# A graph layer on one core: the turn of the values ahead of layer one, the gelu's copy ahead of the signs, and register loads under the last update

## The chip, the cores and the metric

The kernel runs on one core of one Trainium2 chip. The metric is the device time of one execution in microseconds (us). A core has five engines that run side by side, each through its own instruction stream: TensorE (PE, matmuls), VectorE (DVE), ScalarE (ACT), GpSimd (POOL) and SyncE (SP). They meet only at semaphores: an instruction can wait until a semaphore has reached a value, and everything behind it on the same engine waits with it.

## The reference

6250 nodes with 256 features each, 100,000 edges sorted by their row node. With `xn = layernorm(x)` the reference computes

```python
# graph attention, with L0_gnn_W_w, W_b, a_w, a_b; row = src, col = dst
Wh = xn @ W_w + W_b
e  = f_dst_part[col] + f_row_part[row] + a_b[0];  e = where(e > 0, e, 0.2 * e)
m  = segment_max(e, row);  ex = exp(e - m[row]);  denom = segment_sum(ex, row)
h  = relu(segment_sum((ex / denom[row])[:, None] * Wh[col], row))
# linear attention with 8 heads: q, k = elu(.) + 1, context = k^T v, out @ Wproj^T + bproj
x  = x + h + mix(xn)
# mixture of experts on layernorm(x): router, softmax, top 2 of 8, and for every expert
h = gelu(tokens @ w1[e] + b1[e]);  y = h @ w2[e] + b2[e];  out = out + combine[:, e:e+1] * y
x  = x + moe(layernorm(x))
```

All eight experts are computed for every token, and the weights of the six that were not chosen are zero.

## The kernel before

**Tiles.** The nodes lie in 49 tiles of 128. `xs` holds x for all of them on chip. The edges are put in the order of their row nodes and cut into 904 tiles of 128, two tiles to a group (452 groups), four groups to a slot (113 slots, `GS` is 4). A prologue (the first layernorm, the projections and the table of `Wh` rows in memory) takes the first 520 us. After it all engines run one loop over slots, written out in full, `for s in range(-2, S_END)`; there are no planner and no scheduler, and the order on each engine is the order in which the loop body calls the functions.

**The graph part of a slot.** POOL gathers the `Wh` rows of every edge tile from the table with an indirect DMA (L640, 904 of them, eight to a slot). The ring `G` has room for 16 groups, so the gather of group g waits until `total(g - 16)` has been done on TensorE (semaphore `e_A`). DVE takes a slot's edge scores (`edge_scores`, L1528 to L1536) as soon as `spread` on TensorE has written them (semaphore `e_EX`), builds the one-hot matrices (L1539), multiplies them by the weights (L1547, L1549) and, for the slot after that, by the values (`values`, L1556, semaphore `e_V`). TensorE turns these values with eight transposes (`turn`, L1049, semaphore `e_VT`). DVE takes their maximum (`shifts`, L1561 and four small ones). ACT makes the signs, which are the turned one-hots (`one_hot_turned`, L762, semaphore `e_OT`). TensorE spreads the row quantities over the edges (`spread`, L1067 and L1068), which ends in `e_EX`, and so lets DVE begin the next slot. `total(g)` (L1081 to L1083, six matmuls) sums a group's rows; the slot has two of them at its beginning and two in its middle. DVE adds each to the running sum `U` (`add_up`, L1583). Where a node tile has had its last group, `window_end` divides `U` and adds it to `x`, and reads from tables of numbers which node tile is next and at which group it ends (registers `wid` and `last_group`). There are 49 such ends.

**The expert part.** From slot 50 to slot 153 every slot also has one layer one (`up`, L1215, 12 matmuls of 512 columns) of one expert for four node tiles. ACT takes the gelu of both halves (`hidden`, L843; a table load of the activation engine comes ahead of it), copies it to 16 bits (`hidden_hi`, L851, semaphore `m_hi`), and DVE subtracts the copy from the gelu (`split`, L1745). In the slot after, TensorE does layer two (`down`, L1228 and L1231, in two halves), and in the one after that DVE adds the result (`add`, L1758). In slots 50 to 110 both parts run side by side (61 slots); from slot 111 on only the expert part is left.

Two waits stand at the front of `up`: its operands and the gelu of the slot before (`m_g`). `turn` waits for `e_V`, and the two `total` behind both wait for nothing of this slot.

Of the kernel before, what the change touches and what calls it, by code (L numbers as in the profile page):

```python
# [27 lines left out]
ds = bass.ds  # L28


def graph_layer(nc, x, src, dst, W_w, W_b, a_w, a_b, Wq, Wkv, Wproj, bproj, router_w, w1, b1, w2, b2, out):
# [50 lines left out]
    with ExitStack() as ctx:  # L82
# [562 lines left out]
        def _(act):  # L645
# [212 lines left out]
            for s in range(-2, S_END):  # L858
# [13 lines left out]
                if s in UP_AT:  # L872
                    hidden(*UP_AT[s])
                if s + 2 < NS:
                    one_hot_turned(s + 2)
                    if s in UP_AT:
                        act.activation(ready[:, s:s + 1], epsc[:, :], ACT.Exp)
                if s in UP_AT:
                    hidden_hi(*UP_AT[s])
# [20 lines left out]
        def _(pe):  # L900
# [335 lines left out]
            for s in range(-2, S_END):  # L1236
# [15 lines left out]
                if s in FIRST:  # L1252
                    logits(FIRST[s], s)
                if s in UP_AT:
                    up(*UP_AT[s])
                if s + 2 < NS:
                    turn(s + 2)
# [22 lines left out]
        def _(dve):  # L1280
# [8 lines left out]
            def pause():  # L1289

                dve.memset(idle[:, :], 0.0)
# [227 lines left out]
            dve.reg_load(wid, wids[0:1, 0:1])  # L1519
# [3 lines left out]
            link(dve.memset(mx[:, 1, GS:GS + 1], 0.0))  # L1523

# [61 lines left out]
            def window_end(g):  # L1586

                with dve.If(dve.snap(last_group) == g + 1):
                    w = dve.snap(window, min_val=0, max_val=W - 1)
                    dve.wait_ge(e_U, g + 1)  # L1590
# [8 lines left out]
                    dve.wait_ge(f_x, w + 1)  # L1599
                    pause()  # L1600
                    dve.reg_load(last_group, tendi[0:1, ds(w + 1, 1)])
                    dve.reg_load(wid, wids[0:1, ds(w + 1, 1)])
                    dve.reg_add(window, window, 1)

# [50 lines left out]
            def mixed(p):  # L1655
                n = of_pair[p]
                x_p = xs[:, 2 * p:2 * p + n, :]
                dve.wait_ge(a_pj, p + 1)
                dve.tensor_tensor(x_p, x_p, bank[7][:, 0:n * D].rearrange("p (j c) -> p j c", j=n), ALU.add
                                  ).then_inc(a_x, 1)  # L1660
                dve.wait_ge(a_x, p + 1)


            def norm_stats(b):
                n = of_batch[b]
                for j in range(n):
                    rest(5 * b + j)
                    dve.reg_load(wid_n, wids[0:1, b * NB + j:b * NB + j + 1])
                    x_w = xs[:, ds(dve.snap(wid_n, min_val=0, max_val=W - 1), 1), :].rearrange("p a c -> p (a c)")
                    dve.bn_stats(stats[:, j, :], x_w).then_inc(m_st, 1)  # L1670
# [178 lines left out]
```

## Time and profile before

| | |
|---|---|
| median of 3 runs | 2242.29 us (2235.94 to 2250.9) |
| profiled execution | 2250.89 us |
| its span | 2249.1 us |
| TensorE busy | 1711.7 us (76%) |
| VectorE busy | 1676.1 us (75%) |
| ScalarE busy | 963.0 us (43%) |
| GpSimd busy | 985.1 us (44%) |
| chain that ended last | DVE 41%, PE 25%, issue 17%, unknown queue 8%, ACT 5% |

The profiled execution is the slowest of the three; device time and span differ by 1.8 us. Busy shares are averages over stages that differ: a prologue to about 520 us, slots with graph work alone to 1219 us, slots with graph and expert work to 2004 us, and expert work alone to the end. "remote" as the end of an idle time says that the semaphore came from something the profile doesn't name; "issue" says that nothing visible was waited for.

### The profile page before, as it was taken

Reading aid. Unit: us, or ns where it says so; the run is one execution under the profiler, and the core shown is the slowest. Engines: PE = TensorE matmul, PEld = TensorE weight load, DVE = VectorE, ACT = ScalarE, POOL = GpSimd, SP = SyncE. Lnnn points to the kernel's source line nnn. Section 1 sums busy time; section 2 is a strip of 40 time slices with the busy share of each in tenths; the row PEclk is TensorE's granted clock in tenths of the full one; section 3 lists DMA queues with packets and bytes.
Section 4 is the critical chain, followed back from the end, with each engine's and each line's share of the span. In section 5 each row is a group of like instructions: output and inputs, shape, how many; then the busy total and the mean of one; then the engine's idle time right before and its main releaser. Section 6 shows DMA issues by size and latency. Waiting matters only on the chain.

```text
span 2249.1 us, 40227 instructions
## 1 busy us (share of the span) xinstructions
PE 1711.7 (76%) x13588; PEld 1261.0 (56%) x13588; DVE 1676.1 (75%) x4219; ACT 963.0 (43%) x2291; POOL 985.1 (44%) x988
## 2 busy tenths in 40 slices
PE   3778875641887578888856888887878788889998
PEld 2557562531765466666634555655555555566666
DVE  5999898652666667786667888888788878875665
ACT  6322130211332232222224656565656566656555
POOL 3000003325666666665666666665666656610000
PEclk7899997875999788888877999999999999989999
DMA  5011120113655344433333333333332334930000
GB/s 171 18 55 61 43 72 22 55 44 89 174 162 156 100 124 118 108 101 93 88 83 89 84 91 86 93 84 91 79 93 79 93 78 90 81 40 10 11 20 12
DMA packets 121460, 182.21 MB, mean 81 GB/s; under 512 B 21490, under 2 KB 91902, under 8 KB 121214
## 3 DMA queue, kind: packets, MB, share of 16 engines
q0 software_dynamic: 45312, 120.06, 23.0%
q1 hardware_dynamic: 75904, 59.25, 8.4%
q8 instruction: 111, 1.82, 0.3%
q14 instruction: 133, 1.09, 0.2%
HBM read 152.43 MB, written 26.63 MB: 80 GB/s over the span
## 4 chain that ended last, share of the span: by engine, by line
DVE 41%; PE 25%; issue 17%; another core or an unknown queue 8%; ACT 5%; DVEq 2%; POOL 1%; ACTq 0%; DMA 0%; SPq 0%; POOLq 0%
PE bank L1215 6%; PE bank L1231 5%; DVE mloc L1561 4%; DVE big L1478 3%; DVE scr L1583 3%; DVE big L1745 3%; DVE big L1483 3%; DVE big L1480 2%; DVE work L1758 2%; DVE big L1485 2%; DVE scr L1443 2%; DVE work L1539 2%; DVE work L1556 1%; PE bank L1049 1%
## 5 line engine op out<-in xcount | busy, mean ns | idle before, releaser
L640 POOL DMA_INDIRECT work<-table,tiles x904 | 911.9, 1009 | 573.9 <-PE bank L1083 299.5
L1231 PE MATMUL bank<-big 128*128 128x256 f16 x2352 | 329.9, 281 | 24.5 <-issue 23.2
L1081 PE MATMUL bank<-work,scr 128*128 128x257 f16 x904 | 270.0, 299 | 24.3 <-issue 14.2
L1215 PE MATMUL bank<-scr,big 128*128 128x512 f16 (+1 forms) x1248 | 277.0, 371 | 0.6 <-ACT big L843 0.3
L1082 PE MATMUL bank<-work,scr 128*128 128x256 f16 x904 | 270.6, 299 | 7.0 <-issue 6.6
L1231 PEld LDWEIGHTS bank<-big 128*128 128x128 f16 x2352 | 235.4, 100 | 67.0 <-issue 31.3
L1083 PE MATMUL bank<-work,scr 128*128 128x257 f16 x904 | 268.7, 297 | 3.7 <-issue 3.5
L1583 DVE SCALAR_TENSOR_TENSOR scr<-scr,gg,bank 128x257 f32<-128x257 f32 x452 | 216.6, 479 | 51.3 <-remote 19.1
L762 ACT ACTIVATE work<-bank 128x1024 f16<-128x1024 f16 x113 | 115.7, 1024 | 310.6 <-DVE mloc L1561 211.3
L972 PE MATMUL bank<-big 128*128 128x208 f16 x1568 | 176.9, 268 | 73.1 <-DVE big L1485 54.8
L972 PEld LDWEIGHTS bank<-big 128*128 128x128 f16 x1568 | 150.5, 102 | 99.4 <-issue 94.1
L1049 PE MATMUL bank<-identh,work 128*128 128x128 f16 x904 | 79.3, 239 | 156.8 <-DVE work L1556 109.8
L1745 DVE TENSOR_TENSOR big<-big 128x1024 f16<-128x1024 f32 (+1 forms) x104 | 120.8, 1161 | 100.2 <-ACT big L851 86.5
L1215 PEld LDWEIGHTS bank<-scr,big 128*128 128x128 f16 x1248 | 118.1, 98 | 123.7 <-issue 9.9
L843 ACT ACTIVATE big<-bank,b1c 128x512 f32<-128x512 f32 (+1 forms) x208 | 126.6, 659 | 134.2 <-PE bank L1215 111.3
L1758 DVE SCALAR_TENSOR_TENSOR work<-bank,comb,work 128x256 f32<-128x256 f32 x392 | 169.1, 477 | 7.9 <-issue 7.3
L1049 PEld LDWEIGHTS bank<-identh,work 128*128 128x128 f16 x904 | 62.4, 108 | 188.6 <-DVE work L1556 124.5
L1561 DVE TENSOR_REDUCE mloc<-bank 128x4 f32<-128x1024 f16 x113 | 137.7, 1219 | 35.0 <-PE bank L1049 20.6
L1067 PE MATMUL bank<-tiles,work 128*128 128x2 f16 x904 | 60.3, 165 | 95.9 <-ACT work L762 51.0
L745 ACT ACTIVATE w<-s 128x8 f32<-128x8 f32 x113 | 23.5, 208 | 254.7 <-DVE s L1536 211.9
L1228 PE MATMUL bank<-big,onesq 128*128 128x256 f16 x392 | 109.6, 279 | 23.0 <-DVE work L1758 15.1
L691 ACT COPY big<-bank 128x256 f32<-128x256 f32 x49 | 18.3, 373 | 252.3 <-PE bank L984 230.9
(342 smaller groups left out, 3416.6 us busy)
## 6 DMA issues: line engine op xcount, KB each, us to landing
work<-table,tiles POOLq DMA_INDIRECT x904
scr<-normed_cols SPq DMA_DIRECT2D x98, 128.0 KB
table<-big SPq DMA_DIRECT2D x49, 129.0 KB, 2.2
normed_rows<-scr SPq DMA_DIRECT2D x49, 128.5 KB, 2.8
big<-normed_rows SPq DMA_DIRECT2D x49, 128.5 KB
normed_cols<-big SPq DMA_DIRECT2D x49, 128.0 KB, 1.7
xs<-in_x_dram SPq DMA_DIRECT2D x4, 1536.0 KB, 14.5
out_dram<-work SPq DMA_DIRECT2D x48, 128.0 KB
```

Source lines behind the costliest of these rows:

```text
L640: pool.indirect_dma_start(G[:, r, j, :], None, table, bass.IndirectOffsetOnAxis(ap=col[:, t:t + 1], axis=0)).then_inc(rows_in[r // GS], 16)
L972: mm = pe.matmul(bank[4 + k][:, 0:TT], A[n % 2][:, j // 2, :, j % 2], Bh[n % 2][:, j // 2, :, j % 2], start=(n == BATCH[b] and j == 0), st ...
L1049: mm = pe.transpose(VT[:, j * P:(j + 1) * P], V[:, j // 2, :, j % 2], identh[:, :])
L1081: pe.matmul(of[:, 0:D + 1], hi, Gh[:, r, j, 0:D + 1], start=(j == 0), stop=False)
L1082: pe.matmul(of[:, 0:D], hi, Gh[:, r, j, D + 2:2 * D + 2], start=False, stop=False)
L1083: mm = pe.matmul(of[:, 0:D + 1], lo, Gh[:, r, j, 0:D + 1], start=False, stop=(j == GT - 1))
L1215: mm = pe.matmul(bank[5 + f][:, 0:n * P], w1p[pw][:, e, h, f * P:(f + 1) * P], x2p[b % 2][px][:, h, 0:n * P], start=(h + m == 0), stop=(h ...
L1231: mm = pe.matmul(of, hTp[ph][:, k % 2, f, (j + c) * P:(j + c + 1) * P], w2p[pw][:, e, f, :], start=False, stop=(f == 1 and m == 2))
L1561: dve.tensor_reduce(mloc[:, :], VT.rearrange("p (k e) -> p k e", k=GS), AX.X, ALU.max).then_inc(e_ml, 1)
L1583: dve.scalar_tensor_tensor(U, U, gg[:, g // GS % 4, g % GS:g % GS + 1], bank[3 + g % 2][:, 0:D + 1], ALU.mult, ALU.add).then_inc(e_U, 1)
L1745: dve.tensor_tensor(hTp[1][:, k % 2, :, 0:n * P], hT[:, :, 0:n * P], hTp[0][:, k % 2, :, 0:n * P], ALU.subtract).then_inc(m_lo, 1)
L1758: ins = dve.scalar_tensor_tensor(a_, bank[Y_BANK[i % 2]][:, c * D:(c + 1) * D], comb[:, b % 2, j + c, e:e + 1], a_, ALU.mult, ALU.add)
```

## The change

Three orders are changed, and no arithmetic.

1. ACT copies the gelu (`hidden_hi`) right behind `hidden`, ahead of the signs and of the small Exp, which is there to have its table loaded.
2. TensorE turns the values (`turn(s + 2)`) ahead of layer one (`up`).
3. In `window_end` the two register loads, and the small memset ahead of them (`pause`), go to the start of the branch, where the last update of `U` still runs. The wait for the addition to `x`, at the end of the branch so far, is gone from there: it stands at the branch's start for the addition before, and in `mixed` (25 calls) and `norm_stats` (13 calls), which read `x`, as `windows_added`. A memset at the start gives `f_x` its first count, and `reg_load(wid, ...)` ahead of the loop is gone.

```diff
--- before.py
+++ after.py
@@ -871,12 +871,11 @@
                     norm_scale(FIRST[s + 4])
                 if s in UP_AT:
                     hidden(*UP_AT[s])
+                    hidden_hi(*UP_AT[s])
                 if s + 2 < NS:
                     one_hot_turned(s + 2)
                     if s in UP_AT:
                         act.activation(ready[:, s:s + 1], epsc[:, :], ACT.Exp)
-                if s in UP_AT:
-                    hidden_hi(*UP_AT[s])
                 if s - 2 in A_AT:
                     reciprocals_sb(A_AT[s - 2])
                 for p in K_AT.get(s, ()):
@@ -1251,10 +1250,10 @@
                     norm_turned(FIRST[s + 1], len(halves(FIRST[s + 1])) - 1, s)
                 if s in FIRST:
                     logits(FIRST[s], s)
+                if s + 2 < NS:
+                    turn(s + 2)
                 if s in UP_AT:
                     up(*UP_AT[s])
-                if s + 2 < NS:
-                    turn(s + 2)
                 if 0 <= s < NS:
                     for g in range(GS * s + GS // 2, GS * (s + 1)):
                         total(g)
@@ -1516,11 +1515,11 @@
             window = dve.alloc_register("window")
             wid = dve.alloc_register("wid")
             wid_n = dve.alloc_register("wid_n")
-            dve.reg_load(wid, wids[0:1, 0:1])
             dve.reg_mov(window, 0)
             dve.reg_load(last_group, tendi[0:1, 0:1])
             link(dve.memset(U, 0.0))
             link(dve.memset(mx[:, 1, GS:GS + 1], 0.0))
+            dve.memset(started[:, 3:4], 0.0).then_inc(f_x, 1)
 
             def edge_scores(s):
                 dve.wait_ge(e_EX, s + 1)
@@ -1587,6 +1586,10 @@
 
                 with dve.If(dve.snap(last_group) == g + 1):
                     w = dve.snap(window, min_val=0, max_val=W - 1)
+                    pause()
+                    dve.reg_load(wid, wids[0:1, ds(w, 1)])
+                    dve.reg_load(last_group, tendi[0:1, ds(w + 1, 1)])
+                    dve.wait_ge(f_x, w + 1)
                     dve.wait_ge(e_U, g + 1)
                     dve.tensor_scalar(dn[:, :], U[:, D:D + 1], 1e-30, None, ALU.max).then_inc(f_dn, 1)
                     dve.wait_ge(f_dn, w + 1)
@@ -1596,11 +1599,11 @@
                     dve.wait_ge(f_hh, w + 1)
                     x_w = xs[:, ds(dve.snap(wid, min_val=0, max_val=W - 1), 1), :].rearrange("p a c -> p (a c)")
                     dve.tensor_tensor(x_w, x_w, hh, ALU.add).then_inc(f_x, 1)
-                    dve.wait_ge(f_x, w + 1)
-                    pause()
-                    dve.reg_load(last_group, tendi[0:1, ds(w + 1, 1)])
-                    dve.reg_load(wid, wids[0:1, ds(w + 1, 1)])
                     dve.reg_add(window, window, 1)
+
+            def windows_added():
+
+                dve.wait_ge(f_x, dve.snap(window, min_val=0, max_val=W) + 1)
 
             def keys_one(p):
                 n = of_pair[p]
@@ -1655,6 +1658,7 @@
             def mixed(p):
                 n = of_pair[p]
                 x_p = xs[:, 2 * p:2 * p + n, :]
+                windows_added()
                 dve.wait_ge(a_pj, p + 1)
                 dve.tensor_tensor(x_p, x_p, bank[7][:, 0:n * D].rearrange("p (j c) -> p j c", j=n), ALU.add
                                   ).then_inc(a_x, 1)
@@ -1663,6 +1667,7 @@
 
             def norm_stats(b):
                 n = of_batch[b]
+                windows_added()
                 for j in range(n):
                     rest(5 * b + j)
                     dve.reg_load(wid_n, wids[0:1, b * NB + j:b * NB + j + 1])
```

On ACT, in a slot that has both parts (`ready<-epsc` is the small Exp, `work<-bank` the signs, CAST the copy of the gelu). Before:

```order
L843 ACTIVATE big<-bank,b1c 128x512 [waits m_up]
L843 ACTIVATE big<-bank,b1c 128x512
L762 ACTIVATE work<-bank 128x1024 [waits e_EX,e_ml]
L877 ACT_TABLE_LOAD
L877 ACTIVATE ready<-epsc 128x1
L851 CAST big<-big 128x1024 [waits m_y,m_g]
L745 ACTIVATE w<-s 128x8 [waits e_S,e_s3]
```

and now:

```order
L843 ACTIVATE big<-bank,b1c 128x512 [waits m_up]
L843 ACTIVATE big<-bank,b1c 128x512
L851 CAST big<-big 128x1024 [waits m_y,m_g]
L762 ACTIVATE work<-bank 128x1024 [waits e_EX,e_ml]
L878 ACT_TABLE_LOAD
L878 ACTIVATE ready<-epsc 128x1
L745 ACTIVATE w<-s 128x8 [waits e_S,e_s3]
```

The copy has moved up by three rows, and the signs now stand behind it.

On TensorE, in the middle of such a slot, between the second `total` and the third. Before:

```order
L1083 MATMUL bank<-work,scr 128x257
L1215 MATMUL bank<-scr,big 128x512 [waits m_g,m_xlo]
L1215 MATMUL bank<-scr,big 128x512 x11
L1049 MATMUL bank<-identh,work 128x128 [waits e_OT,e_ml,e_V]
L1049 MATMUL bank<-identh,work 128x128 x7
L1081 MATMUL bank<-work,scr 128x257 [waits e_U,e_S]
```

and now (lines are one lower from here on):

```order
L1082 MATMUL bank<-work,scr 128x257
L1048 MATMUL bank<-identh,work 128x128 [waits e_OT,e_ml,e_V]
L1048 MATMUL bank<-identh,work 128x128 x7
L1214 MATMUL bank<-scr,big 128x512 [waits m_g,m_xlo]
L1214 MATMUL bank<-scr,big 128x512 x11
L1080 MATMUL bank<-work,scr 128x257 [waits e_U,e_S]
```

The transposes, with their wait for `e_V`, now stand ahead of layer one, and the third and fourth `total` are still behind both.

On DVE, behind the update that a node tile ends with (the branch is taken 49 times). Before:

```order
L1588 COMPARE_AND_BRANCH
L1591 TENSOR_SCALAR dn<-scr 128x1
L1592 REGISTER_ALU
L1593 RECIPROCAL rd<-dn 128x1
L1595 TENSOR_SCALAR work<-scr,rd 128x256
L1597 ISA
L1598 TENSOR_TENSOR xs<-xs,work 128x256
L1291 MEMSET idle 128x1
L1601 ISA
L1601 TENSOR_LOAD tendi
L1602 REGISTER_ALU
L1602 TENSOR_LOAD wids
```

and now:

```order
L1587 COMPARE_AND_BRANCH
L1290 MEMSET idle 128x1
L1590 ISA
L1590 TENSOR_LOAD wids
L1591 ISA
L1591 TENSOR_LOAD tendi
L1594 TENSOR_SCALAR dn<-scr 128x1
L1596 RECIPROCAL rd<-dn 128x1
L1598 TENSOR_SCALAR work<-scr,rd 128x256
L1600 ISA
L1601 TENSOR_TENSOR xs<-xs,work 128x256
```

Memset and loads have moved from behind the addition to `xs` to ahead of the first small operation.

## Rows read from the trace of the kernel before

**Rows 1.** The three later stages (window: length, busy by engine, granted clock, DMA share, GB/s).
```profile
524.00:1219.00 695.00, 508.89 (x3709) 393.16 (x3710) 461.67 (x1162) 193.10 (x565) 429.69 (x424) 0.83 0.42 115
1219.00:2004.00 785.00, 633.40 (x5479) 447.37 (x5477) 654.24 (x1769) 482.16 (x935) 470.68 (x468) 0.94 0.40 85
2004.00:2249.00 245.00, 232.00 (x1815) 164.19 (x1813) 149.55 (x410) 142.85 (x212) 0.00 (x0) 0.99 0.04 12
```

**Rows 2.** DVE's edge operation: first and last of 62 starts that bound 61 slots.
```profile
1212.45 0.17 DVE L1528 TENSOR_TENSOR s<-bank,work 128x8 f32<-128x8 f32 x1 [0.87 <-issue]
...
2009.29 0.16 DVE L1528 TENSOR_TENSOR s<-bank,work 128x8 f32<-128x8 f32 x1
```

**Rows 3.** DVE groups, 1219 to 2004 us: busy, mean ns, idle before and its releasers.
```profile
L1583 DVE SCALAR_TENSOR_TENSOR scr<-scr,gg,bank 128x257 f32<-128x257 f32 x240 | 114.9, 479 | 23.0 <-issue 11.4 <-remote 5.4 <-PE bank L1083 2.7
...
L1561 DVE TENSOR_REDUCE mloc<-bank 128x4 f32<-128x1024 f16 x61 | 74.3, 1217 | 22.7 <-PE bank L1049 14.3 <-remote 5.8 <-issue 2.5
L1745 DVE TENSOR_TENSOR big<-big 128x1024 f16<-128x1024 f32 x60 | 73.3, 1221 | 23.4 <-issue 12.8 <-ACT big L851 9.9
```

**Rows 4.** One slot on DVE (start, length, engine, line, idle before).
```profile
1341.71 0.17 DVE L1528 TENSOR_TENSOR s<-bank,work 128x8 f32<-128x8 f32 x1 [0.23 <-remote]
...
1344.13 0.68 DVE L1556 TENSOR_TENSOR work<-work,fdp 128x1024 f16<-128x1024 f16 x1
...
1347.96 1.22 DVE L1561 TENSOR_REDUCE mloc<-bank 128x4 f32<-128x1024 f16 x1 [1.45 <-remote]
...
1352.72 1.23 DVE L1745 TENSOR_TENSOR big<-big 128x1024 f16<-128x1024 f32 x1 [0.90 <-ACT big L851]
1354.05 0.17 DVE L1528 TENSOR_TENSOR s<-bank,work 128x8 f32<-128x8 f32 x1
```

**Rows 5.** The same slot on TensorE.
```profile
1342.43 2.75 PE L1215 MATMUL bank<-scr,big 128*128 128x512 f16 x12
1345.02 0.61 PE L1049 MATMUL bank<-identh,work 128*128 128x128 f16 x8
...
1346.69 0.27 PE L1083 MATMUL bank<-work,scr 128*128 128x257 f16 x1
...
1350.69 0.16 PE L1068 MATMUL bank<-tiles,work 128*128 128x2 f16 x1
```

**Rows 6.** The same slot on POOL: first and last gather of its two bursts.
```profile
1342.20 0.96 POOL L640 DMA_INDIRECT work<-table,tiles  x1 [1.68 <-PE bank L1083]
...
1346.00 0.96 POOL L640 DMA_INDIRECT work<-table,tiles  x1 [0.30 <-issue]
1348.27 0.95 POOL L640 DMA_INDIRECT work<-table,tiles  x1 [1.31 <-PE bank L1083]
...
1352.05 0.96 POOL L640 DMA_INDIRECT work<-table,tiles  x1 [0.30 <-issue]
```

**Rows 7.** The same slot on ACT.
```profile
1345.22 1.27 ACT L843 ACTIVATE big<-bank,b1c 128x512 f32<-128x512 f32 x2 [0.37 <-PE bank L1215]
1349.22 1.02 ACT L762 ACTIVATE work<-bank 128x1024 f16<-128x1024 f16 x1 [2.73 <-issue]
...
1351.66 1.03 ACT L851 CAST big<-big 128x1024 f16<-128x1024 f32 x1
```

**Rows 8.** Two transposes of the values on TensorE behind long idle times.
```profile
1539.83 0.57 PE L1049 MATMUL bank<-identh,work 128*128 128x128 f16 x7 [3.58 <-DVE work L1556]
...
1685.11 1.03 PE L1049 MATMUL bank<-identh,work 128*128 128x128 f16 x8 [4.03 <-DVE work L1556]
```

**Rows 9.** The end of a node tile on DVE.
```profile
1557.94 0.06 DVE L1291 MEMSET idle<- 128x1 f32 x1
1558.87 1.23 DVE L1745 TENSOR_TENSOR big<-big 128x1024 f16<-128x1024 f32 x1 [0.87 <-issue]
```

**Rows 10.** The register loads of one line (times in ns: least, median, most).
```profile
L1601 DVEq TENSOR_LOAD <-tendi x49: 301/309/319, 583.5 to 1941.6; - x49
```

**Rows 11.** A slot of the stage before: last gather and next edge operation.
```profile
762.90 0.95 POOL L640 DMA_INDIRECT work<-table,tiles  x1 [0.30 <-issue]
765.37 0.17 DVE L1528 TENSOR_TENSOR s<-bank,work 128x8 f32<-128x8 f32 x1 [3.14 <-remote]
```

## The prediction, made before the changed kernel ran

> **What bounds the kernel now.** I read the times by stage first [rows 1]. The tail of experts alone has TensorE busy 232 of 245 us at a granted clock of 0.99, and the change only touches its order of copies, so it stays. The stage of slots 50 to 110 is where all three edits meet, and there no engine is full: DVE is busy 654 of 785 us, TensorE 633. So the time of a slot is set by a loop through several engines. Its length is read between two edge operations of DVE (L1528): 2009.29 - 1212.45 = 796.8 us for 61 slots, 13.06 us each [rows 2].
>
> Next, where DVE idles in that stage [rows 3]: 22.7 us ahead of the maximum of the turned values (L1561), of them 14.3 for the transposes; 23.4 us ahead of the split (L1745), of them 9.9 for the copy on ACT. These are the waits that edits 1 and 2 aim at. The 12.8 us "issue" there and 11.4 ahead of L1583 hold the register loads of edit 3.
>
> Then one slot on four engines. In it DVE's edge operation starts at 1341.71; call that e. The values end at e + 3.10 [rows 4]. TensorE, meanwhile, runs `up` from e + 0.72 to about e + 3.3, so it fills just the time in which the values are made, and its transposes start at e + 3.31 and are followed by the last `total`, ending at e + 5.25 [rows 5]. POOL has made four gathers, stopped, starts the other four at e + 6.56 and the last at e + 10.34 [rows 6]. The `spread` that the next edge operation waits for ends at 1350.85 (e + 9.14) [rows 5], but DVE does not begin before 1354.05, e + 12.34, which is 2.00 us after the start of the last gather [rows 4, 6]. In this slot DVE has a late split in between, so I look at one without experts: 762.90 is the last gather, 765.37 the edge operation, with DVE idle for 3.14 us ahead of it and `spread` long over [rows 11]. Over the stage, 37 edge operations come in a pause between two bursts of gathers; 29 of these start 2.0 to 2.8 us behind the start of the last gather, 5 sooner, 3 later. The others come while a burst runs, at the end of DVE's own work. I take it as this: **what TensorE signals reaches the others only about 2 us after the start of the last gather of a burst**. The trace shows the times, not the mechanism.
>
> **Edit 2, the turn ahead of layer one.** It removes from the transposes the wait for `up`, and adds to `up`, and to both `total` behind it, the wait for `e_V`. From the slot above: the values are there at e + 3.10. The transposes need 0.45 until the next matmul can start (1345.02 to 1345.47, of 0.61 in all) [rows 5], `up` 2.59 (1342.43 to 1345.02), and the third `total` about 0.8. The third `total` ends at 3.10 + 0.45 + 2.59 + 0.8 = e + 6.9, the fourth near 7.6, against 5.25 now. TensorE stands still from about e + 0.4 to e + 3.1, where it did `up` before. Gathers restart at about e + 7.4 instead of 6.56; the last of the four starts 3 x 1.26 = 3.78 later, at 11.2; with 2.0 more the next edge operation is at **e + 13.2**. No slot with four gathers behind the third `total` can be shorter.
>
> How much that costs depends on how many slots are shorter now. Of the 61 lengths, whose ends are in [rows 2], 34 are below 13.2 (the shortest 10.55), and raising these to 13.2 gives 42.4 us; to 13.7, 60.8 us (43 slots); to 14.0, 74.3.
>
> The granted clock pushes upward. Ten times in this stage the transposes stand behind at least 2.2 us of idle TensorE; six of these ran at the full clock, as after 3.58 us idle, and four at half of it, 1.03 us instead of 0.61 [rows 8]. The change makes such an idle time in nearly every slot. Where the transposes run at the half clock (1.2 instead of 2.4 GHz) they lose 0.42 us, and some of `up` behind them up to as much as its own length, 2.6. With four in ten, and 0.4 to 2 us each, the mean is 0.2 to 0.8; I take 0.5, and so 13.7 us: **+61 us**, with bounds +42 (full clock always) and +119 (14.9 us, half clock in every slot for most of `up`).
>
> The Trainium skill, "TensorE: Matmul & The Clock Gate", the section on HAM oscillation, says of a loop in which each step computes for a short while and then waits that the engine starts cold at every step. The rows agree only in part: four of ten.
>
> **Edit 1, the copy ahead of the signs.** Copy 1.03 us, signs 1.02, table load and Exp 1.4 between them [rows 7]. The copy is ready 2.4 us earlier behind the gelu. The gelu now starts with `up` at about e + 6.2 and ends at e + 7.5 to 7.8, the copy at 8.9, the signs at 9.9, `spread` near 10.5. The split at 9.9 finds its copy. The signs were ready to go at e + 5.9 and are pushed back by 3 us; that costs nothing as long as 10.5 is ahead of 13.2, and if the gathers did not hold the edge operation, it would be behind a DVE chain of 10.55 by little. So the edit is worth at most the 9.9 us of waits for the copy [rows 3], and only in slots that the floor above does not set.
>
> The same goes for the waits for the transposes, 14.3 us. If 18 of 61 slots are longer than 13.7, the share of both is (14.3 + 9.9) x 18 / 61 = **-7 us**.
>
> **Edit 3, the register loads.** Behind a node tile's addition come the memset and 0.87 us in which DVE does nothing [rows 9]; in it lie two loads of 0.31 [rows 10]. Under the update (0.48 us) they hide in part: bounds 0 and -0.93, and I take -0.4, since a load pair is longer than what is left of the update when the branch is decided. Some 24 of the 49 ends lie before slot 50 and 25 in the stage. In the slots without experts DVE waits for the edge operation anyway, 3.14 us in the one shown [rows 11], so few of them count: -2. In the stage 18/61 of 25 ends: 7 x 0.4 = **-3 us**. The 38 new waits for the last addition find it done; 0 to +0.1 each, taken as 0. What covers them is the same wait on edges.
>
> The Trainium skill, "DMA: Bandwidth & Descriptors", in "Latency and other measured facts", gives a floor of about 600 ns for one `tensor_load`; the rows have 0.31. By its figure an end would give 1.2 instead of 0.6 us of loads, an estimate; the trace decides.
>
> **Sum.** 61 - 7 - 3 - 2 = +49 us. On the profiled execution 2250.9 + 49 = 2300; that execution is the slowest of three, and against their median it is 2242.3 + 49 = 2291, rounded to **2292 us**. The bounds of this case alone: +28 (full clock, 42 less 14) to +70, that is 2270 to 2312.
>
> **Rivals.**
> *A, faster: nothing holds the edge operation.* If the 2 us behind the gathers are a coincidence of DVE's own work, only the waits count. The maximum finds its values turned (-14.3 and half the remote 5.8), the split its copy (-9.9, of which the later gelu gives back half), and 25 window ends give 10: about -28, **2214 us**. It decides if edge operations can start, in most slots, at less than 1.5 us behind the last gather of a burst. For it: the five that do, and the 24 that come while a burst runs. Against it: the 29, and the slot in which DVE is empty and `spread` done [rows 11]. Chance 0.17.
>
> *B, the same: gain and loss meet.* The floor is 13.2 at full clock or less, because the third `total` alone restarts POOL earlier than I put it (at e + 7.0, 16.6 to 29.8 us for floors of 12.3 to 12.8), and the waits of all longer slots go, with -12 to -20. This gives 0 to +18: **2250 us**. Chance 0.2.
>
> *C, the clock falls in every slot.* In the stage without experts, with TensorE busy 509 of 695 us, the clock is 0.83 against 0.94 [rows 1]. If the idle time of every slot brings the half clock for the turn and for most of `up`, the slot is 14.9 us: +119 - 5, **2355 us**. Against it: the six transposes at full clock. Chance 0.1.
>
> **Numbers.** Forecast 0.53, A 0.17, B 0.2, C 0.1. 1% of 2242 is 22 us, about what a measurement of this kernel can tell from no change: 2220 to 2265. Faster gets A less a little at its edge, 0.16; the same gets B's greater part and the edges of A and the forecast, 0.2; slower the rest, 0.64. The range of 8 in 10 runs from 2220, at the inner edge of A, to 2342, short of C.
>
> **What would show it.** In the trace of the changed kernel: the stage takes about 835 us instead of 785, with the same busy times. Transposes start 0.1 us after the values, behind 2.5 to 3 us of idle TensorE that names L1555 or so as releaser, over 130 us in the stage. L1560, the maximum, waits for next to nothing. The first gather of the second burst starts near e + 7.4, and the edge operation 2.0 to 2.7 us after the last. The stage's clock falls from 0.94 to 0.88 to 0.92. The prediction is wrong if edge operations come without regard to the gathers, if POOL's second burst still starts near e + 6.6, or if the slots that are longer than 13.7 us now shrink by more than the 10 us I give them.

## The result, and the profile after

The changed kernel takes **2293.78 us** (median of 6 runs, 2276.84 to 2306.23) against 2240.69 us (6 runs, 2235.94 to 2259.52) for the kernel before in the same comparison: ratio 1.0213, interval 1.0181 to 1.0245. It is slower beyond its interval; whether by more or by less than 2% the interval doesn't decide. The profiled execution has a span of 2304.5 us, 55.4 more than before. Ratios are of undisturbed executions: one of the eleven of the changed kernel run again later took 3179 us and is not in its ratio.

The time is in the stage in which graph and expert work meet. Windows of the changed kernel, as in [rows 1] (window: length, busy PE, PEld, DVE, ACT, POOL, granted clock, DMA share, GB/s):

```profile
524.00:1219.00 695.00, 508.66 (x3708) 394.36 (x3707) 463.36 (x1167) 193.06 (x566) 430.31 (x425) 0.83 0.42 115
1219.00:2060.00 841.00, 654.42 (x5487) 449.93 (x5486) 655.01 (x1771) 482.85 (x936) 468.53 (x468) 0.91 0.37 79
2060.00:2304.00 244.00, 230.88 (x1810) 163.01 (x1807) 147.22 (x403) 142.17 (x211) 0.00 (x0) 1.00 0.04 12
```

The stages around it have hardly moved: 2.2 us less up to the first of the edge operations below, 1.9 us more behind the last. DVE and ACT have the same busy time, TensorE has 21 us more at a clock of 0.91 instead of 0.94. The edge operations that bound the 61 slots, to compare with [rows 2]:

```profile
1210.26 0.17 DVE L1527 TENSOR_TENSOR s<-bank,work 128x8 f32<-128x8 f32 x1 [1.91 <-remote]
...
2062.77 0.17 DVE L1527 TENSOR_TENSOR s<-bank,work 128x8 f32<-128x8 f32 x1 [0.31 <-PE bank L1067]
```

852.5 us instead of 796.8, that is 13.98 us for a slot instead of 13.06: +55.7, the whole loss. DVE's groups in this stage (busy, mean ns, idle before and releasers), the same lines as in [rows 3] and the edge operation:

```profile
L1582 DVE SCALAR_TENSOR_TENSOR scr<-scr,gg,bank 128x257 f32<-128x257 f32 x241 | 115.6, 480 | 60.1 <-PE bank L1082 49.6 <-remote 7.3 <-issue 0.7
...
L1750 DVE TENSOR_TENSOR big<-big 128x1024 f16<-128x1024 f32 x60 | 73.1, 1219 | 5.3 <-ACT big L851 4.3
L1560 DVE TENSOR_REDUCE mloc<-bank 128x4 f32<-128x1024 f16 x60 | 72.9, 1216 | 2.6 <-remote 2.6
...
L1527 DVE TENSOR_TENSOR s<-bank,work 128x8 f32<-128x8 f32 x60 | 9.9, 166 | 69.8 <-remote 53.0 <-PE bank L1067 16.6
```

The waits that the change aims at are gone: 22.7 to 2.6 ahead of the maximum, 23.4 to 5.3 ahead of the split. Two others have taken their place: the updates of `U` wait 60.1 us (23.0 before), 49.6 of it for a `total`, and the edge operation waits 69.8.

There are two kinds of slot now (e is again the start of the slot's edge operation). In the first TensorE keeps its full clock. Turn and layer one; then the last gather of the first burst, and the first and last of the second; then DVE's edge operations:

```profile
1421.90 0.62 PE L1048 MATMUL bank<-identh,work 128*128 128x128 f16 x8 [1.86 <-DVE work L1555]
1422.36 2.76 PE L1214 MATMUL bank<-scr,big 128*128 128x512 f16 x12
```

```profile
1423.63 0.95 POOL L640 DMA_INDIRECT work<-table,tiles  x1 [0.30 <-issue]
1426.05 0.95 POOL L640 DMA_INDIRECT work<-table,tiles  x1 [1.47 <-PE bank L1082]
...
1429.83 1.55 POOL L640 DMA_INDIRECT work<-table,tiles  x1 [0.30 <-issue]
```

```profile
1418.69 0.17 DVE L1527 TENSOR_TENSOR s<-bank,work 128x8 f32<-128x8 f32 x1 [1.95 <-remote]
...
1431.84 0.17 DVE L1527 TENSOR_TENSOR s<-bank,work 128x8 f32<-128x8 f32 x1 [1.29 <-remote]
```

The second burst starts at e + 7.36, the last gather at e + 11.14, the next edge operation at e + 13.15, 2.01 us behind it. In the second kind the clock falls in the wait for the values:

```profile
1355.38 1.03 PE L1048 MATMUL bank<-identh,work 128*128 128x128 f16 x8 [2.50 <-DVE work L1555]
1356.21 5.21 PE L1214 MATMUL bank<-scr,big 128*128 128x512 f16 x12
```

Layer one takes 5.21 us instead of 2.76. On ACT the gelu, the copy and the signs follow it in a row, and on DVE the edge operation starts at 1366.61, 14.34 us after the one at 1352.27, released by the `spread` (L1067) and not by a gather (the last one started at 1366.19):

```profile
1361.46 1.26 ACT L843 ACTIVATE big<-bank,b1c 128x512 f32<-128x512 f32 x2 [6.05 <-PE bank L1214]
1362.76 1.05 ACT L851 CAST big<-big 128x1024 f16<-128x1024 f32 x1
1363.71 1.02 ACT L762 ACTIVATE work<-bank 128x1024 f16<-128x1024 f16 x1
```

```profile
1366.61 0.17 DVE L1527 TENSOR_TENSOR s<-bank,work 128x8 f32<-128x8 f32 x1 [1.54 <-PE bank L1067]
```

It comes 1.27 us after the end of this `spread`. In ten of the 61 slots it is 1.27 to 1.35 us behind it, so in them the 2 us behind the last gather are not what DVE waits for.

Both traces have the same 61 slots, so each can be set beside itself. Layer one takes more than 3.2 us in 32 of them (5 before). These 32 took 406.9 us and take 461.3: 12.71 us each before, 14.42 now, +54.5 in sum. The other 29 took 390.0 and take 391.2: 13.45 each before, 13.49 now, +1.2. So nearly the whole loss lies in the slots in which layer one met the half clock. They were the shorter slots before, so this does not yet say how much of it is the clock and how much the order.

### The profile page after: what moved, and what is told of

Same layout as the page of the kernel before. It is cut to its first block, busy times and chain, and to the rows that moved or that the text cites. A ratio compares the mean times of both kernels' runs of the same rounds, so it can differ in the third digit from the quotient of the medians.

```text
span 2304.5 us, 40290 instructions
## 1 busy us (share of the span) xinstructions
PE 1732.0 (75%) x13588; PEld 1264.4 (55%) x13588; DVE 1675.2 (73%) x4220; ACT 963.0 (42%) x2291; POOL 982.6 (43%) x988
## 4 chain that ended last, share of the span: by engine, by line
DVE 33%; PE 31%; issue 15%; another core or an unknown queue 12%; ACT 5%; DVEq 2%; POOL 1%; ACTq 0%; DMA 0%; SPq 0%; POOLq 0%
PE bank L1214 11%; PE bank L1230 4%; DVE big L1477 3%; DVE mloc L1560 3%; DVE big L1482 2%; PE bank L1048 2%; DVE big L1479 2%; DVE big L1484 2%; DVE work L1555 2%; DVE scr L1582 2%; DVE big L1750 2%; DVE work L1538 2%; PE bank L1134 2%; ACT work L762 2%
## 5 line engine op out<-in xcount | busy, mean ns | idle before, releaser
L1214 PE MATMUL bank<-scr,big 128*128 128x512 f16 (+1 forms) x1248 | 326.3, 419 | 0.4 <-ACT big L843 0.3
L1230 PE MATMUL bank<-big 128*128 128x256 f16 x2352 | 314.9, 274 | 13.8 <-issue 13.5
L1048 PE MATMUL bank<-identh,work 128*128 128x128 f16 x904 | 90.3, 259 | 248.7 <-DVE work L1555 193.7
L1080 PE MATMUL bank<-work,scr 128*128 128x257 f16 x904 | 264.5, 293 | 5.1 <-DVE scr L1582 2.6
L1081 PE MATMUL bank<-work,scr 128*128 128x256 f16 x904 | 265.0, 293 | 2.6 <-issue 2.5
L1082 PE MATMUL bank<-work,scr 128*128 128x257 f16 x904 | 262.8, 291 | 3.7 <-issue 3.7
L1230 PEld LDWEIGHTS bank<-big 128*128 128x128 f16 x2352 | 229.7, 98 | 49.6 <-issue 18.7
L971 PE MATMUL bank<-big 128*128 128x208 f16 x1568 | 175.9, 267 | 72.5 <-DVE big L1484 55.4
L1048 PEld LDWEIGHTS bank<-identh,work 128*128 128x128 f16 x904 | 67.9, 117 | 272.9 <-DVE work L1555 212.2
L1214 PEld LDWEIGHTS bank<-scr,big 128*128 128x128 f16 x1248 | 129.8, 109 | 154.5 <-issue 68.0
L971 PEld LDWEIGHTS bank<-big 128*128 128x128 f16 x1568 | 149.8, 102 | 99.5 <-issue 94.5
L1527 DVE TENSOR_TENSOR s<-bank,work 128x8 f32<-128x8 f32 x113 | 18.6, 165 | 170.9 <-remote 149.0
L1066 PE MATMUL bank<-tiles,work 128*128 128x2 f16 x904 | 60.1, 166 | 90.8 <-ACT work L762 51.8
L1477 DVE TENSOR_TENSOR big<-tiles,scr 128x1664 f16<-128x1664 f16 x98 | 99.9, 1019 | 33.3 <-PE bank L971 18.8
```

Source lines behind the costliest of these rows:

```text
L971: mm = pe.matmul(bank[4 + k][:, 0:TT], A[n % 2][:, j // 2, :, j % 2], Bh[n % 2][:, j // 2, :, j % 2], start=(n == BATCH[b] and j == 0), st ...
L1048: mm = pe.transpose(VT[:, j * P:(j + 1) * P], V[:, j // 2, :, j % 2], identh[:, :])
L1080: pe.matmul(of[:, 0:D + 1], hi, Gh[:, r, j, 0:D + 1], start=(j == 0), stop=False)
L1081: pe.matmul(of[:, 0:D], hi, Gh[:, r, j, D + 2:2 * D + 2], start=False, stop=False)
L1082: mm = pe.matmul(of[:, 0:D + 1], lo, Gh[:, r, j, 0:D + 1], start=False, stop=(j == GT - 1))
L1214: mm = pe.matmul(bank[5 + f][:, 0:n * P], w1p[pw][:, e, h, f * P:(f + 1) * P], x2p[b % 2][px][:, h, 0:n * P], start=(h + m == 0), stop=(h ...
```

## The experiments

They ran on four chips (numbers 0, 2, 5 and 7), and on all of them the kernel before takes **2064 us**, not 2241. The number of the first comparison's chip is not on record. Each run was compared with the kernel before on its own chip. Most of the expectations were written for a kernel of 2241 us, so they are read here as ratios. The first thing to read is therefore the kernel before, traced again on one of them (no edit).

> The kernel before, traced. Where it takes 2064 us, the stage without experts has slots of 11.0 us instead of 12.96, edge operations do not wait 2 us behind the last gather of a burst, and POOL's bursts run into each other; the idle time ahead of the edge operation named remote, 104.6 us in the first trace, is below 10. Where it takes 2240 us, they are as in the first trace.

2061.28 us, a span of 2059.5. The idle time ahead of the edge operation (L1528, whole span), by releaser:

```profile
  issue: 14.6, 17
  PE bank L1068: 1.6, 2
```

No idle time named remote is left there, nor ahead of the edge operation in any other trace of the experiments. Slots take 12.25 us in the mean instead of 13.06, those without experts 11.1 instead of 13.0, and of 61 edge operations two come 1.9 to 2.9 us behind the last gather, where in the first trace it was 30. The very first edge operation shows it best. In the first trace 32 gathers run without a pause, and this is the end of the first `spread`, the last of these gathers, and the edge operation:

```profile
525.77 0.17 PE L1068 MATMUL bank<-tiles,work 128*128 128x2 f16 x1
```

```profile
548.22 0.95 POOL L640 DMA_INDIRECT work<-table,tiles  x1 [0.31 <-issue]
```

```profile
550.91 0.17 DVE L1528 TENSOR_TENSOR s<-bank,work 128x8 f32<-128x8 f32 x1 [25.75 <-issue]
```

and on the other chip, where the gathers go on from 487.7 to beyond 529:

```profile
504.39 0.17 PE L1068 MATMUL bank<-tiles,work 128*128 128x2 f16 x1
```

```profile
504.08 0.95 POOL L640 DMA_INDIRECT work<-table,tiles  x1 [0.30 <-issue]
505.34 1.25 POOL L640 DMA_INDIRECT work<-table,tiles  x1 [0.31 <-issue]
```

```profile
504.59 0.17 DVE L1528 TENSOR_TENSOR s<-bank,work 128x8 f32<-128x8 f32 x1 [0.81 <-PE bank L1068]
```

There it starts 0.03 us after `spread` has ended, in the middle of a burst; in the first trace it comes 25 us after `spread` and 2.7 behind the last gather. So the hold on which the prediction rests belongs to the chip of the first comparison, or to a state it was in; the program is the same. The difference of the two spans, 189.6 us, is 46 to the first edge operation, 94 in the slots without experts, and 49 in the 61 with them.

**The change on such a chip** (no edit).

> The changed kernel itself, on the chips on which the kernel before takes 2064 instead of 2241 us and on which halving the gathers of the kernel before gave nothing. From the parts on those chips (order alone +113 us, copy -23, loads -25): 2064 + 65 = 2110 to 2140 us, 3% slower, more than the 2.1% where edge operations are held behind the gathers. Theory that the second burst of gathers matters there too in the changed kernel (with half the gathers it took 2060): second bursts start at e + 7.3 or e + 8.9, and the next edge operation waits for the totals. If the change cost only through the hold of the edge operation, it would be the same here, 2050 to 2075 us.

2070.73 us (11 runs), ratio 1.0029 (1.0020 to 1.0038). Neither 2110 to 2140 nor its reason came true: the loss is 6 us where edge operations aren't held. That lies in the range given for the case that the change costs only through the hold. But edit 2 costs here too, and edits 1 and 3 pay for it, as the next runs show; the parts do not add up. What DVE waits for in the stage (1067 to 1820 us; us in total, times, longest):

```profile
DVE scr L1582 <- PE bank L1082: 22.7, 25, 2.8
DVE w4l L1543 <- ACT w4h L746: 17.6, 13, 1.9
...
DVE big L1750 <- ACT big L851: 2.8, 9, 0.5
```

**The turn back behind layer one**: edits 1 and 3 stay.

```diff
-                if s + 2 < NS:
-                    turn(s + 2)
                 if s in UP_AT:
                     up(*UP_AT[s])
+                if s + 2 < NS:
+                    turn(s + 2)
```

> Edits 1 and 3 with the turn back behind layer one. My theory (the second burst of gathers waits for the third total, and the edge operation for the gathers): the loss of the change goes wholly, about 2240 less what the waits and the register loads give, so 2215 to 2240 us; POOL's second burst starts at e + 6.6 again. The rival, that the loss comes from the signs behind the copy (spread late, edge operation late): 2275 to 2295 us, as the signs stay where the change has put them.

2019.17 us against 2063.79, ratio 0.9788 (0.9771 to 0.9804). It beats both kernels. As a ratio 0.988 to 1.0 was expected, and it is better. With the full change at 1.0029, edit 2 on top of the other two costs 2.4%, some 50 us. The waits of the same stage:

```profile
DVE dn L1594 <- DVE scr L1582: 9.3, 13, 0.8
DVE xs L1601 <- DVE work L1598: 4.1, 26, 0.2
...
DVE work L1555 <- ACT fdp L754: 3.3, 2, 1.8
DVE mloc L1560 <- PE bank L1048: 1.6, 3, 0.7
```

The updates no longer wait for `total`, and the maximum waits 1.6 us for its transposes, though they stand behind layer one. In the kernel before on such a chip it was only 2.7 us (1067 to 1813 us), against 14.3 on the first chip [rows 3], so on these chips edit 2 had next to nothing to gain:

```profile
L1561 DVE TENSOR_REDUCE mloc<-bank 128x4 f32<-128x1024 f16 x61 | 74.2, 1216 | 2.7 <-PE bank L1049 2.7
```

The weights (L1543) no longer wait for ACT either, which is free earlier.

**Edit 2 alone** in the kernel before.

```diff
-                if s in UP_AT:
-                    up(*UP_AT[s])
                 if s + 2 < NS:
                     turn(s + 2)
+                if s in UP_AT:
+                    up(*UP_AT[s])
```

> The kernel before with edit 2 alone. My theory: the whole loss and a little more, since edits 1 and 3 gain: 2295 to 2310 us. The rival of the late signs: no loss to speak of, 2230 to 2250 us, as the transposes come earlier and the signs stand ahead of the copy.

2176.78 us, ratio 1.0547 (1.0529 to 1.0564), +113 us: more than the whole change, and above the 1.025 to 1.031 expected. Layer one is slow in all 61 slots (more than 3.2 us; 15 in the full change, 2 before, on such chips). One slot, TensorE, ACT and DVE:

```profile
1279.26 0.62 PE L1049 MATMUL bank<-identh,work 128*128 128x128 f16 x8 [1.81 <-DVE work L1556]
1279.72 4.44 PE L1215 MATMUL bank<-scr,big 128*128 128x512 f16 x12
```

```profile
1284.20 1.26 ACT L843 ACTIVATE big<-bank,b1c 128x512 f32<-128x512 f32 x2 [4.35 <-PE bank L1215]
1285.35 1.02 ACT L762 ACTIVATE work<-bank 128x1024 f16<-128x1024 f16 x1
1286.39 1.28 ACT L877 ACT_TABLE_LOAD   x1
1287.69 0.20 ACT L877 ACTIVATE ready<-epsc 128x1 f32<-128x1 f32 x1
1287.80 1.03 ACT L851 CAST big<-big 128x1024 f16<-128x1024 f32 x1
```

```profile
1288.86 1.27 DVE L1745 TENSOR_TENSOR big<-big 128x1024 f16<-128x1024 f32 x1 [2.75 <-ACT big L851]
1290.05 0.15 DVE L1528 TENSOR_TENSOR s<-bank,work 128x8 f32<-128x8 f32 x1
```

From the values to the next edge operation all stands in one row: turn, layer one, gelu, signs, table load, Exp, copy, split, edge operation. DVE then makes the next values 3.1 us after that, TensorE waits for them, 2.8 us in the mean of the 61 slots, and layer one is slow again. Edit 1 takes signs, table load and Exp (2.5 us) out of the row. Edits 1 and 3 together give 2.1% without edit 2 (0.9788) and 5.2% behind it (1.0547 to 1.0029), 107 us. Alone they give 23 and 25 us (below). No run has edits 2 and 3 without edit 1; if edit 3 gave its 1.2% there too, edit 1 would be worth some 80 us behind edit 2, an estimate.

**The same with half the gathers**, to ask whether POOL is on that row. From the seventeenth group on it leaves out one of the two gathers, and that tile keeps the rows of an earlier group.

```diff
-                for j in range(GT):
+                for j in range(GT if g < GR else 1):
...
-                act.wait_ge(rows_in[r // GS], 16 * ST * (GS * s // GR + 1))
+                act.wait_ge(rows_in[r // GS], 16 * (ST + GS * (GS * s // GR)))
```

> Edit 2 alone (turn first, copy still behind signs, table load and Exp), with one gather instead of two for every group from the seventeenth on, so the output is not the reference's. Theory that edit 2 without edit 1 loses through ACT (layer one late, gelu late, and then signs, table load, Exp and copy in a row ahead of the split, which DVE does before the next edge operation): the gathers are not on that path, and where the kernel before takes 2064 us this one stays at 2150 to 2180, as with all gathers (2177). Rival, that it loses through POOL (third total late, second burst late): it falls to 2055 to 2090 us. Where edge operations are held behind the gathers (kernel before 2240), this one falls to 2150 to 2180 us too, 130 us below what edit 2 alone would have there.

2175.33 us, ratio 1.0541 (1.0516 to 1.0565), against 1.0547 with all gathers. The gathers have no part in it here.

**Edit 3 alone** in the kernel before; all of the change to `window_end`, of which this is the core.

```diff
+                    pause()
+                    dve.reg_load(wid, wids[0:1, ds(w, 1)])
+                    dve.reg_load(last_group, tendi[0:1, ds(w + 1, 1)])
+                    dve.wait_ge(f_x, w + 1)
                     dve.wait_ge(e_U, g + 1)
...
-                    dve.wait_ge(f_x, w + 1)
-                    pause()
-                    dve.reg_load(last_group, tendi[0:1, ds(w + 1, 1)])
-                    dve.reg_load(wid, wids[0:1, ds(w + 1, 1)])
```

> The kernel before with edit 3 alone (register loads under the last update). My theory: 0.4 us for those of 49 node tiles whose end is not covered by the wait for the edges, so -3 to -10 us: 2231 to 2238 us. The rival, that the new waits and the loads stand in the way of the division: 2240 to 2250 us.

2039.14 us, ratio 0.9884 (0.9868 to 0.9901): -25 us, 0.5 us for each of the 49 ends, where a ratio of 0.996 to 0.999 was expected. My 0.4 was the right size; that most of them would be covered wasn't so here. On the first chip edit 3 was not run alone.

**Edit 1 alone** in the kernel before.

```diff
                     hidden(*UP_AT[s])
+                    hidden_hi(*UP_AT[s])
...
-                if s in UP_AT:
-                    hidden_hi(*UP_AT[s])
```

> The kernel before with edit 1 alone (copy of the gelu ahead of the signs). My theory: the split waits for nothing (9.9 us of waits gone), the signs start about when they did, since the gelu ends before the maximum: -5 to -15 us, 2225 to 2236 us. The rival of the late signs: +5 to +20 us, 2245 to 2260 us.

2041.24 us, ratio 0.9898 (0.9881 to 0.9916): -23 us, more than the 0.993 to 0.998 expected. The split's wait for the copy was 22.9 us in the traced kernel before; it is 3.2 in all now. The line of the split in this run (1067 to 1800 us):

```profile
L1744 DVE TENSOR_TENSOR big<-big 128x1024 f16<-128x1024 f32 x61 | 74.3, 1219 | 3.2 <-issue 1.8
```

**Layer one behind the third and fourth total.**

```diff
                 if s + 2 < NS:
                     turn(s + 2)
-                if s in UP_AT:
-                    up(*UP_AT[s])
                 if 0 <= s < NS:
                     for g in range(GS * s + GS // 2, GS * (s + 1)):
                         total(g)
+                if s in UP_AT:
+                    up(*UP_AT[s])
```

> The changed kernel with layer one moved behind the third and fourth total: turn, totals, layer one. My theory: the third total ends near e + 4.4, POOL's second burst starts at e + 6.6 as before the change, and the loss goes; the gelu, copy, signs and spread come later, spread at about e + 11.4, which is still ahead of the held edge operation at 12.3, so 2235 to 2260 us. Rival (TensorE's idle time ahead of the turn is what costs, through the clock and through the later layer one): the idle time is the same, so 2280 to 2310 us.

2115.46 us, ratio 1.0240 (1.0216 to 1.0264). My theory said that the loss would go; the ratio lies in the rival's range (1.018 to 1.031). The theory gave no weight to layer one itself being late: the split waits 35.5 us for the copy and the weights 25.0 for ACT. The updates still wait 20.8 us for a `total` (22.7 in the changed kernel), so moving the totals ahead of layer one did not take that wait away. On these chips a late layer one costs through ACT. The clock of the stage is 0.90 instead of 0.96, and no run separates how much of the 49 us is the clock.

**Filler matmuls ahead of the turn** in the changed kernel.

```diff
+            def filler(b, e):
...
+                for i in range(FILL):
+                    pe.matmul(bank[5][:, 0:n * P], w1p[0][:, e, 0, 0:P], x2p[b % 2][0][:, 0, 0:n * P],
+                              start=True, stop=True)
...
+                if s in UP_AT and s + 2 < NS:
+                    filler(*UP_AT[s])
                 if s + 2 < NS:
                     turn(s + 2)
```

`FILL` is 9, and the filler has the two waits of `up`.

> The changed kernel with nine matmuls of 512 columns ahead of the turn in every slot that has layer one, into a bank that layer one overwrites: TensorE is busy for 1.9 us of the 2.7 that it idles there. Theory of two parts (late third total at full clock +42, half clock the rest): the stage's granted clock rises from 0.91 to 0.97 or more, the second burst starts at e + 7.3 in nearly every slot instead of 8.9 or 10.2 in many, and the time falls to 2255 to 2280 us. Rival (the clock costs nothing, all of the loss is the order): 2290 to 2310 us, the same or a little more.

2064.64 us, ratio 1.0004 (0.9994 to 1.0013), against 1.0029 without them on another chip. The stage in this run:

```profile
1067.00:1820.00 753.00, 699.68 (x6103) 484.67 (x6103) 658.31 (x1794) 485.89 (x947) 498.15 (x479) 1.00 0.42 91
```

Neither range came true as a ratio (1.007 to 1.018, and 1.022 to 1.031 for the rival). The clock is at its full rate from end to end, and the whole gives back 5 us. That is not the price of the clock, for the filler costs something itself. Slot by slot, against the changed kernel traced again: in the 15 slots in which layer one was slow there, 169.3 us instead of 194.2; in the other 46, 584.2 instead of 565.4. In the trace the transposes start 0.52 us after the values in the mean, up to 2.2, instead of 0.06. With the turn put back the same slots take 164.1 and 544.5 us. So of the 51 us between the two orders 30 lie in the 15 slots and 21 in the 46. The filler takes away 25 of the 30, which is then about what the half clock costs: half of the 51, and the other half is the order. This is an estimate from one trace each, on three chips.

**Half the gathers** (the diff above) in the changed kernel and in the one before.

> The changed kernel with one gather instead of two for every group from the seventeenth on; the other tile keeps the rows of an earlier group. 436 gathers fewer, so the output is not the reference's. All work of DVE, TensorE and ACT stays. Theory of the gathers (an edge operation comes 2 us after the start of the last one): the last gather of a slot starts 2.5 us sooner, and edge operations come at 10.6 to 12 instead of 14: the 61 slots fall from 852 to 690 to 760 us, the slots without experts from 12.96 to 11 or less, and the whole to 2040 to 2170 us. Rival (nothing is held, and the edge operation waits for spread or for DVE): within 20 us of 2294.

> The same halving of the gathers in the kernel before. Theory of the gathers: here too slots shorten, to DVE's own chain of 10.6 to 12 us each, so 2040 to 2140 us, and the gap between this order and the changed one shrinks from 53 us to less than 25, because what the late third total costs goes through the gathers. Rival (nothing is held): within 20 us of 2240, and the gap stays at 53.

2059.94 us, ratio 0.9975 (0.9962 to 0.9988), and 2059.30 us, 0.9977 (0.9967 to 0.9987). As ratios both are in the rival's range of 20 us, which fits what the trace of the kernel before shows on such a chip: nothing is held. The test was made for the hold, and ran where there is none. POOL isn't wholly without a part, though: the changed kernel gains 0.5% by it (1.0029 to 0.9975), the one before 0.2%, and with half the gathers the two take the same time.

**Layer one cut in two**: first half, turn, second half.

```diff
-                if s + 2 < NS:
-                    turn(s + 2)
-                if s in UP_AT:
-                    up(*UP_AT[s])
+                if s in UP_AT:
+                    up(*UP_AT[s], (0,))
+                if s + 2 < NS:
+                    turn(s + 2)
+                if s in UP_AT:
+                    up(*UP_AT[s], (1,))
```

> The changed kernel with layer one cut in two: its first half (six matmuls) ahead of the turn, its second behind it. TensorE works for 1.3 us of the time in which it waited for the values, the third total ends 1.3 us earlier (e + 5.6 at the full clock), and the transposes still start with the values. Theory of the late third total and the half clock: the loss goes, 2010 to 2040 us where the kernel before takes 2064, as good as the turn put back (2019) or better by up to 10. Rival (any layer one behind the turn costs, since the gelu and the copy come late): 2060 to 2100 us.

2030.03 us, ratio 0.9837 (0.9822 to 0.9851), in the range expected, but not as good as the turn put back (0.9788), which it was to reach or to beat. What it still waits for in the stage is again behind layer one: 8.0 us for the weights, 2.8 for the totals.

## Why the prediction was right, and where it was not

**The sum** said 2292 us (+49; 2242.3 + 49 is 2291), and the measurement 2293.8 (+53). The way there was right in the main on the chip of the comparison. That it came out within 2 us is luck, for the six runs go from 2277 to 2306. And it is right for that comparison alone: on chip 0, where edge operations are not held, the same change gives +0.3%. The steps:

- *Slot by slot.* For the 43 slots of up to 13.7 us I took +61, and they grew by 63.6. For the waits and loads in the 18 longer ones I took -7 and -3, and they shrank by 7.9. For the slots before I took -2, and they shrank by 1.7. So these terms hold, and not only their sum.
- *The waits move.* The maximum and the split wait for next to nothing, as forecast; the third total becomes late, TensorE stands idle ahead of the turn for 129 us in sum (over 130 forecast), and the stage takes 841 us for the 835 forecast.
- *The hold behind the gathers.* In the slots at the full clock the second burst was put at e + 7.4 and the edge operation at 13.2; the slot shown has 7.36 and 13.15. 28 of 61 edge operations come 1.9 to 2.9 us behind the last gather, 30 before. That the hold is real there, the first edge operation shows. What makes it stays open: it was absent in all traces of the experiments, so no run could take it away where it is.
- *The floor.* "No slot with four gathers behind the third `total` can be shorter" than 13.2 us was wrong: 15 slots with gathers are, seven of them by more than 0.3 us (the shortest takes 11.55). As a mean it held: 14 slots that were below 13.2 us have layer one at the full clock now; the floor gives them 14.3 us, and they grew by 12.0.
- *The clock.* I gave the half clock 18 us (42 to 61). It is in 32 slots. The 20 of them that were below 13.2 us get 28.0 from the floor and grew by 50.0, so 22.0 stand above it. The longer slots go apart by it too: the 15 at the full clock shrank by 10.8, the 12 at the half clock grew by 4.5. So this term was undersized, but only somewhat.
- *The register loads* were not run alone on that chip; the stages before and after move by about 2 us, as forecast. On the others they give 25 us.
- *Rival A*, faster for want of a hold, has its condition fulfilled on the chips of the experiments and its price wrong: there the change is at +0.3%, not at -1.2%. It counted the waits that go and no cost of a late layer one.

The Trainium skill, "TensorE: Matmul & The Clock Gate", the section on HAM oscillation, says that a loop which computes for a short while and then waits starts cold at each step. The trace agrees in part. Of 28 turns behind at least 2.2 us of idle time 16 began at the half clock, more than my four in ten, and layer one behind the turn was slow in 32 of 61 slots; with edit 2 alone it was slow in all 61. For `tensor_load` the Trainium skill, "DMA: Bandwidth & Descriptors", in "Latency and other measured facts", has a floor of about 600 ns. The trace has 0.31 us for each, and -25 us over 49 ends is 0.5 an end, which fits two loads at 0.31 better than two at 0.6; the measurement decides.

Not shown: how the loss on the first chip splits between order and clock. It rests on one trace of each kernel and on the floor, not on a run, and the half clock came in the slots that were short before.

## What to carry to other kernels

When an instruction is moved ahead of another on an in-order engine, price what the other one loses: layer one filled exactly the time in which the values were made, and moving it behind the wait made TensorE idle for 1.9 to 2.8 us a slot in the mean and everything that hangs on layer one late. Of three edits made together, two gave -2.1% and the third took it all back; each has to be run alone and left out alone, for edits 1 and 3 were worth 2.1% without edit 2 and 5.2% behind it. When two traces have the same slots, compare each slot with itself and not with the mean: here that put the loss into 32 slots and showed that the filler, meant to price the clock, cost 19 us of its own. And a wait that ends with nothing the profile can name may be that of the chip or its state and not the program's: trace the kernel before again where the experiments run.

## What the runs showed of the hardware

- One and the same kernel took 2241 us in the first comparison and 2064 on each of four chips. In the first, half of DVE's edge operations (30 of 61) started only 1.9 to 2.9 us after the start of the last gather that GpSimd had issued, and 2.0 us or more after the end of the `spread` that they wait for, 20 of them behind an idle DVE; the first of all came 25 us after it, at the end of unbroken gathers. On the other chip whose trace was taken without an edit, the first came 0.03 us after the signal, in the middle of a burst.
- In the changed kernel of the first comparison, 28 turns of the stage came behind 2.2 us of idle TensorE or more, and 16 of them began at the half clock. With edit 2 alone layer one ran slow in all 61 slots (4.1 us in the mean instead of 2.8), also in the 22 whose turn had less than 2.2 us of idle TensorE ahead of it.
- Nine matmuls of 512 columns in each of these waits kept the granted clock of the stage at 1.00 (0.96 without them).
